# The weighting of the value rows in the softmax pass, moved from VectorE to GpSimd

## The chip, the cores and the metric

The kernel runs on one core of one Trainium2 chip. The metric is the device time of one execution in microseconds (us). A core has TensorE (PE), VectorE (DVE), ScalarE (ACT), GpSimd (POOL) and SyncE (SP, which only issues transfers here). Each engine takes its own instructions in order; engines wait for each other through semaphores. A row that begins with an engine's name and a small q (DVEq) shows the sequencer of that engine, which reads loop bounds, works out addresses and issues instructions.

## The reference, cut to what matters

A graph network over 6250 nodes and 200,000 edges that are sorted by their destination. Two convolutions come first, then attention over the edges, whose last part the change touches:

```
logits = (q[dst] * k[src]).sum(-1) * scale + (edge_attr @ ew + eb)   # 8 heads
amax = segment_max(logits, dst)
pe = exp(logits - amax[dst])
ssum = segment_sum(pe, dst)
w = pe / clip(ssum[dst], 1e-06)
o = segment_sum(w[:, :, None] * v[src], dst)                          # 8 heads x 16 columns
```

## The kernel before, in words

The kernel is a row of phases with a barrier of all engines between them: projection, convolution, node update, the same again, the projection to q, k and v, `logits_pass`, `node_maxima`, `softmax_pass`, and a last node update. The change is in `softmax_pass`, which takes the edges 512 at a time: 392 groups ("supers") of `TILES` = 4 tiles of 128 edges. The division by `ssum` is left to the last node update, so the pass sums `exp * v` (128 columns) and `exp` (8 columns) by destination node.

All engines run the same loop, written by `slots`: one turn for each super, four turns written out in an iteration (`DEPTH` = 4), so that every fourth turn has the loop's branch ahead of it. I call four turns a lap. The stages of one super lie in different turns: with lag 1 TensorE finds the maxima of its nodes, with lag 2 VectorE subtracts them, with lag 3 ScalarE takes the exponential, with lag 4 the value rows are multiplied by it, and with lag 5 the products are summed by node. An engine is in the turn that its own waits allow, so ScalarE may take the exponential of a super right after VectorE's subtraction.

What each engine does in a turn, in its order:

- TensorE: for each block of 128 nodes that the super of lag 5 touches, eight recorded matmuls (L743, four products of 128x136 in f32, each in two parts) of the one-hot matrix `hot` with `vals`; a small matmul (L749) that marks `vals` as read; then the maxima of the super of lag 1 (L1500, L663 for each block, L1504).
- VectorE: reads the super's first and last block into registers (L580, L598); for each block builds `hot` (L708, is_equal of `node_row` and `dst_cols`, both in SBUF) and adds the sums of the block before from PSUM to `acc` (L729); then reduces the maxima from PSUM (L1551), subtracts them from `logits` (L1553, both inputs in SBUF), and multiplies the value rows by their weights (L1559, `vals` from `v` and the last 8 columns of `vals`, all in SBUF).
- ScalarE: the exponential into the last 8 columns of `vals` (L1520), then for each block two passes that make the one-hot matrix `pick` for the maxima (L644, L648).
- SyncE: loads `dst` (a buffer is free when `picked` says so) and `v` (free when `vals` says so), four buffers each.
- GpSimd: one iota at the start of the pass and nothing more.

Two supers are in the sums at a time: `hot` and the PSUM bank of the sums are double. A super whose edges end in another block than they began in has two blocks (there are 47 of these); its second product waits for the second `hot` and for L729, which wait for the first product.

The semaphores that the change touches are `weight` (the exponential is there), `v_in` (the value rows have landed) and `vals` (the product is there: TensorE and SyncE wait for it).

Of the kernel before, what the change touches and what calls it, by code (L numbers as in the profile page):

```python
# [27 lines left out]
ALU = mybir.AluOpType  # L28
# [3 lines left out]
P = 128  # L32
N_NODES, N_EDGES, D = 6250, 200000, 128
HEADS, GROUPS, ED, TD = 8, 8, 4, 512
HD = D // HEADS
# [3 lines left out]
TILES = 4  # L39
# [9 lines left out]
ACC_W = D + HEADS  # L49
# [60 lines left out]
def build(nc, io, out):  # L110
    ctx = ExitStack()
    with ctx:
# [1323 lines left out]
        def softmax_pass():  # L1436

            with ExitStack() as st:
# [9 lines left out]
                dst, v = deep("dst", [P, SUPER]), deep("v", [P, TILES, D])  # L1448
                apart, picks = b("apart", [P, SUPER]), Picks("sm", b("pick", [P, 2, SUPER], BF16))
                zeros = b("zeros", [2, TILES * 3 * HEADS], BF16)  # L1450
                below, highest, vals = b2("below", [P, TILES * HEADS]), b2("highest", [P, TILES * HEADS]), deep("vals", [P, TILES, ACC_W])
# [8 lines left out]
                MAXIMUM, BELOW, LOAD_V, EXPONENT, WEIGHT, SCATTER = 1, 2, 2, 3, 4, 5  # L1460
                with nc.Block() as block:
                    @block.sync
                    def _(sp):
                        def body(stage):
                            if stage(0):
                                s, r, k = stage(0)
                                hold(sp, S["picked"], s - (DEPTH - 1), S["sp_paced"])
                                sp.dma_start(dst[r][:, :], dst_rows[bass.ds(s, 1), :].to_broadcast([P, SUPER])).then_inc(S["dst_in"][r], 16)
                            if stage(LOAD_V):
                                s, r, k = stage(LOAD_V)  # L1470

                                hold(sp, S["vals"], s - (DEPTH - 1), S["sp_paced"])
                                sp.dma_start(v[r][:, :, :], v_edges[bass.ds(s, 1), :, :].rearrange("a p (j c) -> (a p) j c", c=D)).then_inc(S["v_in"][r], 16)
                        slots(sp, LOAD_V, body)

                    @block.gpsimd
                    def _(pool):
                        number_nodes(pool, None, node_row, S["nodes"])

                    @block.tensor  # L1480
                    def _(pe):
                        picked, scattered = picks.counters(pe), scatter.counters(pe)
                        kept = span_registers(pe, "sm")

                        pe.wait_ge(S["set"], 1)
                        pe.matmul(bank(SUMS[0])[:, 0:ACC_W], hot[0][:, 0, :], vals[0][:, 0, :], start=True, stop=True).then_inc(S["sums"], 1)

                        def body(stage):

                            far = stage(SCATTER) and kept_span(pe, kept[stage(SCATTER)[1]])  # L1490
                            near = stage(MAXIMUM) and keep_span(pe, kept[stage(MAXIMUM)[1]], span("pe", stage(MAXIMUM)[0])[0])
                            if stage(SCATTER):
                                s, r, k = stage(SCATTER)
                                scatter.products(pe, scattered, far, r, vals[r], (S["vals"], s + 1))
                            if stage(MAXIMUM):
                                s, r, k = stage(MAXIMUM)

                                wait(pe, S["below"], s - 1)
                                maxima = bank(MAX[r % 2])[:, 0:TILES * 3 * HEADS]
                                pe.matmul(maxima, digit_w[:, :], zeros[:, :], start=True, stop=False, skip_group_check=True)  # L1500
                                pick_pe(pe, picks, picked, near, maxima.rearrange("p (j c) -> p j c", c=3 * HEADS),
                                        lambda blk: [max_parts[:, bass.ds(blk, 1), :, :].rearrange("p a k c -> p (a k c)")])

                                pe.matmul(maxima, digit_w[:, :], zeros[:, :], start=False, stop=True,  # L1504
                                          skip_group_check=True).then_inc(S["maxima"], 1)
                        slots(pe, SCATTER, body)

                    @block.scalar
                    def _(act):
                        picked = picks.counters(act)  # L1510
                        act.sem_inc(picks.made, 1)

                        def body(stage):
                            ends = stage(0) and span("act", stage(0)[0])[0]
                            if stage(EXPONENT):
                                s, r, k = stage(EXPONENT)
                                act.wait_ge(S["below"], s + 1)

                                wait(act, S["vals_free"], s - (DEPTH - 1))
                                act.activation(vals[r][:, :, D:ACC_W], below[r % 2][:, :].rearrange("p (j h) -> p j h", h=HEADS),  # L1520
                                               ACT.Exp).then_inc(S["weight"], 1)
                            if stage(0):
                                s, r, k = stage(0)
                                pick_act(act, S, picks, picked, ends, dst[r][:, :], apart[:, :], (S["dst_in"][r], 16 * (k + 1)))
                                act.sem_inc(S["picked"], 1)
                        slots(act, EXPONENT, body)

                    @block.vector
                    def _(dve):
                        scattered, before = scatter.counters(dve), [counter(dve, f"sm_before_{x}", 0) for x in ("block", "bank")]  # L1530
                        dve.sem_inc(picks.used, 2)
                        number_nodes(None, dve, node_row, S["nodes"])
                        dve.memset(vals[0][:, :, :], 0.0)
                        dve.memset(hot[0][:, :, :], 0.0)
                        dve.memset(zeros[:, :], 0.0).then_inc(S["set"], 1)
                        dve.memset(acc[:, :, :], 0.0).then_inc(S["sums_free"], 1)
                        dve.wait_ge(S["sums_free"], 1)

                        def body(stage):
                            if stage(SCATTER):  # L1540
                                s, r, k = stage(SCATTER)
                                scatter.names(dve, scattered, before, span("dve", s)[0], s, r, node_row)
                            if stage(BELOW):
                                s, r, k = stage(BELOW)
                                dve.wait_ge(S["maxima"], s + 1)

                                wait(dve, S["weight"], s - 1)
                                maxima = bank(MAX[r % 2])[:, 0:TILES * 3 * HEADS].rearrange("p (j k h) -> p j k h", k=3, h=HEADS)
                                under = below[r % 2][:, :].rearrange("p (j h) -> p j h", h=HEADS)

                                dve.tensor_reduce(highest[r % 2][:, :], maxima.rearrange("p j k h -> p j h k"), AX.X, ALU.add).then_inc(S["maxima_used"], 1)  # L1551
                                dve.wait_ge(S["maxima_used"], s + 1)
                                dve.tensor_tensor(under, logits[:, bass.ds(s, 1), :].rearrange("p a (j h) -> p (a j) h", h=HEADS),  # L1553
                                                  highest[r % 2][:, :].rearrange("p (j h) -> p j h", h=HEADS), ALU.subtract).then_inc(S["below"], 1)
                            if stage(WEIGHT):
                                s, r, k = stage(WEIGHT)
                                dve.wait_ge(S["weight"], s + 1)
                                dve.wait_ge(S["v_in"][r], 16 * (k + 1))
                                dve.tensor_tensor(vals[r][:, :, 0:D].rearrange("p j (h c) -> p j h c", c=HD),  # L1559
                                                  v[r][:, :, :].rearrange("p j (h c) -> p j h c", c=HD),  # L1560
                                                  vals[r][:, :, D:ACC_W].unsqueeze(3).to_broadcast([P, TILES, HEADS, HD]),
                                                  ALU.mult).then_inc(S["vals"], 1)
                        slots(dve, SCATTER, body)
                        q = value(dve, scattered[0], 1)
                        dve.wait_ge(S["sums"], q)
                        scatter.add(dve, q, before)
# [59 lines left out]
```

## Time and profile before

| | |
|---|---|
| time, median of 3 runs | 8547.21 us (8544.19 to 8551.21) |
| the profiled execution: time / span | 8545.18 / 8543.4 us |
| busy, share of the span | PE 75%, DVE 65%, POOL 54%, ACT 54% |
| softmax pass | from about 7010 to 8416 us |
| in it: PE / DVE / ACT / POOL busy | 1193.87 / 843.32 / 721.02 / 0.00 us of 1406 |
| granted TensorE clock in it | 0.50 of full speed |

Shares of the whole span mix phases with different limits, and GpSimd's 54% lies in the gathers of the convolutions and of the logits pass. The softmax pass has to be read by itself, turn by turn.

### The profile page before, as it was taken

To read this page: it belongs to the slowest core of one execution; us is meant where nothing else is said; L and a number is where in the kernel's file an instruction comes from. 1 tells how busy PE (TensorE), PEld (TensorE's weight loads), DVE (VectorE), ACT (ScalarE), POOL (GpSimd) and SP (SyncE) were. 2 spreads that over 40 slices of the span, in tenths; PEclk is the share of its full clock that TensorE was granted. 3 is DMA by queue.
4 is the path that set the end of the run, shared out by engine and by line. 5 is a ranking of instruction groups with operands and counts; after the bars stand their busy time and mean duration, and the time that the engine had idled before them with its cause. 6 is when DMAs were issued, how large, how long until landed. Compare 5 with 4: busy or idle time off the path is not lost. (4 is left out here: it accounts for less than half of the span.)

```text
span 8543.4 us, 249109 instructions
## 1 busy us (share of the span) xinstructions
PE 6370.7 (75%) x43500; PEld 4258.2 (50%) x43501; DVE 5559.4 (65%) x14407; ACT 4605.3 (54%) x7842; POOL 4629.7 (54%) x4730
## 2 busy tenths in 40 slices
PE   1788888888648888888884677777666658888884
PEld 1455555555435555555553434343333337776664
DVE  5667676777656666677776566666666666665556
ACT  3445555555334555555552567777777765555542
POOL 0777777777427777777772477777666520000000
PEclk9999999999869999999996655555555555555555
DMA  4445445555225445445451577777666545444442
GB/s 151 134 135 134 135 134 133 134 135 134 73 62 135 134 133 135 135 134 133 134 134 45 162 214 217 215 215 204 194 184 178 167 121 167 156 148 143 135 133 74
DMA packets 1002205, 1233.71 MB, mean 144 GB/s; under 512 B 305427, under 2 KB 647422, under 8 KB 1000674
## 3 DMA queue, kind: packets, MB, share of 16 engines
q1 hardware_dynamic: 776358, 718.99, 28.5%
q0 software_dynamic: 225792, 514.10, 22.5%
q8 instruction: 20, 0.33, 0.0%
q14 instruction: 35, 0.29, 0.0%
HBM read 1091.01 MB, written 141.49 MB: 144 GB/s over the span
## 5 line engine op out<-in xcount | busy, mean ns | idle before, releaser
L823 POOL DMA_INDIRECT conv_rows<-src_table,conv_idx x3136 | 3105.4, 990 | 955.2 <-issue 919.4
L1243 POOL DMA_INDIRECT lg_rows<-kv_table,lg_idx x1568 | 1482.8, 946 | 792.8 <-issue 594.2
L663 PE MATMUL ps<-dst_parts,lg_pick 128*128 x5268 | 668.3, 304 | 671.9 <-ACT lg_pick L648 668.0
L743 PEld LDWEIGHTS ps<-conv_vals,conv_hot 128*128 128x128 f32 x7024 | 916.0, 191 | 504.9 <-issue 349.7
L743 PE MATMUL ps<-sm_vals,sm_hot 128*128 128x136 f32 x3512 | 952.2, 452 | 202.9 <-DVE acc L729 137.7
L887 ACT ACTIVATE conv_sq<-ps 128x512 f32<-128x512 f32 x784 | 468.1, 597 | 1108.2 <-PE ps L853 1010.0
L663 PEld LDWEIGHTS ps<-dst_parts,lg_pick 128*128 x5268 | 522.1, 132 | 1052.3 <-issue 1021.1
L847 PE MATMUL ps<-conv_rows,ident_b 128*128 128x512 bf16 x2352 | 646.8, 384 | 523.6 <-DMA conv_rows<-src_table,conv_idx 478.3
L926 DVE TENSOR_REDUCE conv_var<-conv_sq 128x32 f32<-128x512 f32 x784 | 536.5, 684 | 760.3 <-ACT conv_sq L887 734.6
L743 PE MATMUL ps<-conv_vals,conv_hot 128*128 128x129 f32 x7024 | 938.6, 276 | 108.8 <-DVE acc L729 104.2
L1391 DVE CUSTOM_DVE_ANT_0 acc<-ps,acc 128x512 f32<-128x512 f32 x976 | 635.4, 689 | 549.9 <-ACT acc L1306 497.5
L743 PEld LDWEIGHTS ps<-sm_vals,sm_hot 128*128 128x128 f32 x3512 | 814.0, 329 | 278.9 <-DVE acc L729 213.7
L648 ACT ACTIVATE conv_pick<-conv_apart,one_col 128x512 f32 x878 | 633.7, 722 | 459.3 <-PE ps L663 307.8
L708 DVE TENSOR_TENSOR conv_hot<-conv_node_row,dst_cols 128x512 f32 (+1 forms) x878 | 605.2, 689 | 386.9 <-PE ps L743 312.8
L1306 ACT ACTIVATE acc<-ps,neg_win 128x512 f32<-128x512 f32 x976 | 622.0, 685 | 384.5 <-issue 330.8
L868 PE MATMUL ps<-conv_y,ident 128*128 128x512 f32 x1568 | 806.7, 596 | 3.6 <-DVE conv_y L956 3.6
L663 PE MATMUL ps<-dst_parts,conv_pick 128*128 x10536 | 768.9, 222 | 8.0 <-issue 3.8
L892 ACT ACTIVATE conv_vals<-ps 128x512 f32<-128x512 f32 x784 | 468.1, 597 | 405.0 <-PE ps L868 404.6
L663 PEld LDWEIGHTS ps<-dst_parts,conv_pick 128*128 x10536 | 610.0, 99 | 114.4 <-issue 24.4
L644 ACT ACTIVATE conv_apart<-conv_dst,neg_node 128x512 f32<-128x512 f32 x878 | 628.0, 715 | 40.0 <-DMA conv_dst<-dst_rows 19.9
L956 DVE TENSOR_TENSOR conv_y<-conv_y,conv_gamma 128x512 f32<-128x512 f32 x784 | 545.0, 695 | 15.0
L949 DVE TENSOR_TENSOR conv_y<-ps,conv_rstd 128x512 f32<-128x512 f32 x784 | 534.1, 681 | 0.1
(223 smaller groups left out, 9447.7 us busy)
## 6 DMA issues: line engine op xcount, KB each, us to landing
conv_dst<-dst_rows SPq DMA_DIRECT2D x784, 256.0 KB
acc<-dst_rows SPq DMA_DIRECT2D x392, 256.0 KB
v_edges<-lg_rows SPq DMA_DIRECT2D x392, 256.0 KB
sm_dst<-dst_rows SPq DMA_DIRECT2D x392, 256.0 KB, 3.3
sm_v<-v_edges SPq DMA_DIRECT2D x392, 256.0 KB, 2.6
conv_rows<-src_table,conv_idx POOLq DMA_INDIRECT x3136
conv_ea<-ea_parts SPq DMA_DIRECT2D x784, 36.0 KB
lg_rows<-kv_table,lg_idx POOLq DMA_INDIRECT x1568
```

Source lines behind the costliest of these rows:

```text
L644: act.activation(apart, dst, ACT.Square, bias=neg_node[:, bass.ds(blk, 1)]).then_inc(picks.apart_made, 1)
L648: act.activation(picks.buffer(act, turn), apart, ACT.Relu, bias=one_col[:, 0:1], scale=-1.0).then_inc(picks.made, 1)
L663: last = pe.matmul(to[:, j, :], names, part, start=False, stop=False, skip_group_check=True)
L708: dve.tensor_tensor(hot[:, :, :], node_row[:, bass.ds(blk, 1), :].to_broadcast([P, TILES, P]), dst_cols[:, bass.ds(TILES * s, TILES)].unsq ...
L743: last = pe.matmul(bank(SUMS[g])[:, 0:self.width], self.hot[g][:, j, :], vals[:, j, 0:self.width], start=(j == 0), stop=(j == TILES - 1))
L823: pool.indirect_dma_start(rows[r][:, j, :], None, src_table, bass.IndirectOffsetOnAxis(idx[r][:, j:j + 1], 0)).then_inc(S["rows_in"][r], 16)
L847: last = pe.matmul(bank(MSG[r]).rearrange("p (j c) -> p j c", c=D), ident_b[:, :], rows[r][:, :, p * D:(p + 1) * D], start=(p == 0), stop= ...
L868: pe.matmul(bank(SHIFT[r % 2]).rearrange("p (j c) -> p j c", c=D), ident[:, :], y[r % 2][:, :, :], start=False, stop=True, skip_group_chec ...
L956: dve.tensor_tensor(y[r % 2][:, :, :], y[r % 2][:, :, :], gamma[:, :].unsqueeze(1).to_broadcast([P, TILES, D]), ALU.mult).then_inc(S["gain ...
L1243: pool.indirect_dma_start(rows[r][:, j, :], None, kv_table, bass.IndirectOffsetOnAxis(idx[r][:, j:j + 1], 0)).then_inc(S["rows_in"][r], 16)
L1306: act.activation(far[h], bank(AGAIN[r % 2]), ACT.Square, bias=neg_win[:, bass.ds(w + h, 1)], scale=PEN).then_inc(S["far"], 1)
L1391: dve.tensor_tensor_reduce(masked[h], bank(SPREAD_TO[r % 2]), far[h], 1.0, NEG, ALU.subtract, ALU.max, top[:, h:h + 1]).then_inc(S["top"], 1)
```

## The change

The multiplication by the weights leaves VectorE's loop and becomes a loop of its own on GpSimd, with the same waits, operands and semaphore. GpSimd runs the stage with the other engines' lag, but nothing else is in its loop.

```diff
@@ pool
 number_nodes(pool, None, node_row, S["nodes"])
+def body(stage):
+    if stage(WEIGHT):
+        s, r, k = stage(WEIGHT)
+        pool.wait_ge(S["weight"], s + 1)
+        pool.wait_ge(S["v_in"][r], 16 * (k + 1))
+        pool.tensor_tensor(vals[r][:, :, 0:D].rearrange("p j (h c) -> p j h c", c=HD),
+                           v[r][:, :, :].rearrange("p j (h c) -> p j h c", c=HD),
+                           vals[r][:, :, D:ACC_W].unsqueeze(3).to_broadcast([P, TILES, HEADS, HD]),
+                           ALU.mult).then_inc(S["vals"], 1)
+slots(pool, WEIGHT, body)
@@ dve, at the end of its turn
-if stage(WEIGHT):
-    s, r, k = stage(WEIGHT)
-    dve.wait_ge(S["weight"], s + 1)
-    dve.wait_ge(S["v_in"][r], 16 * (k + 1))
-    dve.tensor_tensor(vals[r][:, :, 0:D].rearrange("p j (h c) -> p j h c", c=HD),
-                      v[r][:, :, :].rearrange("p j (h c) -> p j h c", c=HD),
-                      vals[r][:, :, D:ACC_W].unsqueeze(3).to_broadcast([P, TILES, HEADS, HD]),
-                      ALU.mult).then_inc(S["vals"], 1)
```

VectorE, in the middle of its loop, from the subtraction of one turn to the `hot` of the next, before:

```order
L1551 TENSOR_REDUCE sm_highest<-ps 128x32
L1553 ISA
L1553 TENSOR_TENSOR sm_below<-logits,sm_highest 128x32
L1558 REGISTER_ALU
L1559 TENSOR_TENSOR sm_vals<-sm_v,sm_vals 128x4x128
L580 ISA
L580 TENSOR_LOAD ranges
L689 ISA
L598 REGISTER_ALU
L598 UNCONDITIONAL_BRANCH
L598 ISA
L708 ISA
L708 TENSOR_TENSOR sm_hot<-dst_parts,dst_cols 128x512
```

The same place now (lines of `softmax_pass` have moved by 11):

```order
L1562 TENSOR_REDUCE sm_highest<-ps 128x32
L1564 ISA
L1564 TENSOR_TENSOR sm_below<-logits,sm_highest 128x32
L580 ISA
L580 TENSOR_LOAD ranges
L689 ISA
L598 REGISTER_ALU
L598 UNCONDITIONAL_BRANCH
L598 ISA
L708 ISA
L708 TENSOR_TENSOR sm_hot<-dst_parts,dst_cols 128x512
```

The multiplication and a register instruction are gone; the sequencer's work between the subtraction and `hot` is all still there.

GpSimd's loop of the softmax pass, of which nothing stood before (the iota was followed by the branch to the next phase):

```order
+L1485 TENSOR_TENSOR sm_vals<-sm_v,sm_vals 128x4x128 x4
+L104 UNCONDITIONAL_BRANCH
+L104 ISA
+L1484 REGISTER_ALU
+L1485 TENSOR_TENSOR sm_vals<-sm_v,sm_vals 128x4x128
+L1483 REGISTER_ALU
+L1485 TENSOR_TENSOR sm_vals<-sm_v,sm_vals 128x4x128
+L1483 REGISTER_ALU
+L1485 TENSOR_TENSOR sm_vals<-sm_v,sm_vals 128x4x128
+L1483 REGISTER_ALU
+L1485 TENSOR_TENSOR sm_vals<-sm_v,sm_vals 128x4x128
```

All 392 multiplications are now GpSimd's, and between two of them it has one register instruction and its waits.

## Rows read from the trace of the kernel before

**Rows 1.** Busy time of each engine in the softmax pass, then granted clock and DMA

```profile
7010.00:8416.00 1406.00, 1193.87 (x6436) 984.86 (x6436) 843.32 (x2055) 721.02 (x1266) 0.00 (x0) 0.50 0.45 144
```

**Rows 2.** Groups of instructions, 6700 to 8450: busy, mean ns, idle before, releasers

```profile
L743 PE MATMUL ps<-sm_vals,sm_hot 128*128 128x136 f32 x3512 | 952.2, 452 | 202.9 <-DVE acc L729 137.7 <-issue 42.1 <-DVE sm_vals L1559 15.3
L1559 DVE TENSOR_TENSOR sm_vals<-sm_v,sm_vals 128x512 f32<-128x512 f32 x392 | 270.3, 690 | 0.6 <-issue 0.6
```

**Rows 3.** Timeline of TensorE over one lap (start us, us, instruction)

```profile
7427.39 2.18 PE L743 MATMUL ps<-sm_vals,sm_hot 128*128 128x136 f32 x8 [0.64 <-DVE acc L729]
...
7429.91 0.26 PE L1504 MATMUL ps<-sm_zeros,digit_w 2*128 2x96 bf16 x1
7430.36 2.18 PE L743 MATMUL ps<-sm_vals,sm_hot 128*128 128x136 f32 x8 [0.19 <-DVE acc L729]
...
7432.87 0.26 PE L1504 MATMUL ps<-sm_zeros,digit_w 2*128 2x96 bf16 x1
7433.30 2.17 PE L743 MATMUL ps<-sm_vals,sm_hot 128*128 128x136 f32 x8 [0.17 <-DVE acc L729]
...
7436.12 2.18 PE L743 MATMUL ps<-sm_vals,sm_hot 128*128 128x136 f32 x8
...
7439.51 0.82 PE L743 MATMUL ps<-sm_vals,sm_hot 128*128 128x136 f32 x2 [0.62 <-DVE acc L729]
```

**Rows 4.** Timeline of VectorE over the same lap

```profile
7428.73 0.69 DVE L708 TENSOR_TENSOR sm_hot<-dst_parts,dst_cols 128x512 f32 x1 [0.29 <-issue]
...
7430.54 0.26 DVE L1551 TENSOR_REDUCE sm_highest<-ps 128x32 f32<-128x96 f32 x1 [0.40 <-PE ps L1504]
7430.95 0.19 DVE L1553 TENSOR_TENSOR sm_below<-logits,sm_highest 128x32 f32<-128x32 f32 x1
7431.06 0.69 DVE L1559 TENSOR_TENSOR sm_vals<-sm_v,sm_vals 128x512 f32<-128x512 f32 x1
7432.03 0.69 DVE L708 TENSOR_TENSOR sm_hot<-dst_parts,dst_cols 128x512 f32 x1 [0.28 <-issue]
...
7435.05 0.69 DVE L708 TENSOR_TENSOR sm_hot<-dst_parts,dst_cols 128x512 f32 x1 [0.29 <-issue]
...
7438.27 0.69 DVE L708 TENSOR_TENSOR sm_hot<-dst_parts,dst_cols 128x512 f32 x1 [0.62 <-issue]
```

**Rows 5.** VectorE's sequencer, line 580, from 7431.1 to 7432.3 (ns min/median/max)

```profile
L580 DVEq TENSOR_LOAD <-ranges x1: 301/301/301, 7431.2 to 7431.2; - x1
```

**Rows 6.** Timeline of ScalarE over the same lap: the exponentials

```profile
7431.18 0.23 ACT L1520 ACTIVATE sm_vals<-sm_below 128x32 f32<-128x32 f32 x1 [0.24 <-DVE sm_below L1553]
...
7434.27 0.23 ACT L1520 ACTIVATE sm_vals<-sm_below 128x32 f32<-128x32 f32 x1 [0.37 <-DVE sm_below L1553]
...
7437.41 0.23 ACT L1520 ACTIVATE sm_vals<-sm_below 128x32 f32<-128x32 f32 x1 [0.56 <-DVE sm_below L1553]
```

**Rows 7.** Timeline of all engines at the second block of a super

```profile
8318.73 0.69 DVE L708 TENSOR_TENSOR sm_hot<-dst_parts,dst_cols 128x512 f32 x1 [2.44 <-PE ps L743]
...
8319.68 2.18 PE L743 MATMUL ps<-sm_vals,sm_hot 128*128 128x136 f32 x8 [1.14 <-DVE acc L729]
```

**Rows 8.** Timeline of all engines in the first node update

```profile
2294.32 1.72 POOL L1147 TENSOR_TENSOR node_biased<-node_bias,node_held 128x896 f32<-128x896 f32 x1 [40.52 <-DVEq L1090]
...
2294.54 0.20 DVE L1092 RECIPROCAL node_share<-node_share 128x7 f32<-128x7 f32 x1
2294.78 2.21 DVE L1093 TENSOR_TENSOR node_stage<-acc,node_share 128x896 f32<-128x896 f32 x1
...
2304.70 0.17 DVE L1089 TENSOR_SCALAR node_held<-acc 128x7 f32 x1 [0.28 <-DVE node_y L1106]
2305.00 1.68 POOL L1147 TENSOR_TENSOR node_biased<-node_bias,node_held 128x896 f32<-128x896 f32 x1 [8.96 <-DVEq L1090]
2305.02 1.70 DVE L1091 TENSOR_SCALAR node_share<-acc 128x7 f32 x1
...
2307.09 1.09 DVE L1093 TENSOR_TENSOR node_stage<-acc,node_share 128x896 f32<-128x896 f32 x1
```

**Rows 9.** GpSimd's 14 multiplications (ns min/median/max, first and last start)

```profile
L1147 POOL TENSOR_TENSOR node_biased<-node_bias,node_held x14: 1681/1682/1719, 2294.3 to 4661.8; 128x896 f32<-128x896 f32 x14
```

## The prediction

> **What bounds the kernel now.** The change lives in the softmax pass alone, so I read first the busy times of that stretch: TensorE is busy 1193.87 of 1406 us at a granted clock of 0.50 (its 1.2 GHz level), VectorE 843.32, GpSimd not at all [rows 1]. The groups of instructions come next: 3512 recorded parts of products (439 products of eight parts, for 392 supers), 202.9 us of idle time before them, 137.7 of it put down to VectorE's L729; the multiplication that moves is 392 times 690 ns, 270.3 us in all [rows 2]. If those 270 us lay on the path, the kernel would gain 3%. Whether they do is a question for one lap of four turns.
>
> In the lap from 7427.39 to 7439.51, TensorE runs its products (L743) for 2.18 us, then the maxima up to L1504, 2.77 or 2.78 us from the start of L743 to the end of L1504, and begins the next products 0.1 to 0.7 us later; the lap is 12.12 us, 3.03 a turn [rows 3]. Does TensorE wait for anything in those gaps? Its product needs `hot`. At a second block, where it surely waits, L743 starts 0.26 us behind the end of `hot` (8319.42 to 8319.68) [rows 7]. In the lap the ends of `hot` lie at 7429.42, 7432.72, 7435.74 and 7438.96 and the products start at 7430.36, 7433.30, 7436.12 and 7439.51 [rows 3, 4]. That is 0.94, 0.58, 0.38 and 0.55 us; less the 0.26, `hot` comes **0.68, 0.32, 0.12 and 0.29 us early**. So nothing of VectorE holds TensorE in these turns, though L729 is named as the releaser: for a first block L743 needs the L729 of the turn before. What sets the pass is TensorE with its own issue gaps, which are long after the loop's branch (0.64) [rows 3]. But VectorE is only a little ahead.
>
> Its chain is this: L1504 ends at 7430.17 [rows 3], the reduction starts at 7430.54, the subtraction at 7430.95, the multiplication at 7431.06, `hot` at 7432.03 [rows 4], and the product that needs it at 7433.30. The chain spans two turns of TensorE, and its margin is the margin above.
>
> **What leaves VectorE.** The multiplication takes 0.69 us, but `hot` starts 0.97 us behind it, and of that 0.28 is marked as issue [rows 4]: the sequencer reads the super's range (a load of 0.30 us that starts at 7431.2) and sets up the loop [rows 5], all of it under cover of the multiplication. The change leaves these instructions where they are. With the multiplication gone the sequencer's work stands bare, so `hot` can start earlier by no more than the step from subtraction to multiplication, 0.11 us (7430.95 to 7431.06) [rows 4]. TensorE, which doesn't wait there, gains nothing from it. Gain: 0.
>
> **What GpSimd gets.** Its price per multiplication: it took 1682 ns for 128x896 f32, two inputs in SBUF, one of them repeated along the row [rows 9]. By size alone, 512 columns are 1682 x 512/896 = 0.96 us. With a fixed part as large as VectorE's (690 ns at 512, 1.09 us at 896, so 1.04 ns a column and 0.155 us fixed [rows 2, 8]) it is 1.03. I take **0.99**, well under a turn of 3.03: throughput is no issue, and `vals` is ready two turns before its product. SyncE's load of `v` waits for `vals`, which now comes earlier.
>
> **What GpSimd does to VectorE.** This is the term that decides. In the node update GpSimd multiplied from 2294.32 to 2296.04; VectorE's reciprocal ran in that time in its 0.20 us, but L1093, with two inputs in SBUF, started at 2294.78 and took 2.21 us, against 1.09 alone: it ended 0.95 us behind GpSimd's end. L1091 took 1.70 us in the next round, from 2305.02 to 2306.72, where GpSimd ended at 2306.68, while L1089 of the same shape took 0.17 [rows 8]. So such an instruction is held until GpSimd's multiplication ends, and is then done in its own time less 0.14 us. The Trainium skill (SBUF — State Buffer, Who interferes with whom) says that a DVE instruction with two SBUF inputs contends with a GpSimd instruction that reads SBUF, and that the one that issues second blocks fully; by that rule, the trace agrees (L1093, 2.21 us). `hot` (L708) and the subtraction (L1553) have two inputs in SBUF; the reduction and L729 read PSUM.
>
> Where does GpSimd's multiplication fall? It starts when the exponential is done: L1089 ended at 2304.87 and GpSimd began at 2305.00, 0.13 us later [rows 8]. The exponentials end at 7431.41, 7434.50 and 7437.64 [rows 6], so GpSimd starts at 7431.54, 7434.63 and 7437.77, ahead of `hot`'s new earliest starts (7431.92, 7434.94, 7438.16), and holds it each time. GpSimd ends 0.99 later, and `hot` 0.55 after that (0.69 less 0.14):
>
> - `hot` of 7432.03: ends at 7433.08, 0.36 late against 7432.72; 0.32 are free; 0.04 too late.
> - `hot` of 7435.05: ends at 7436.17, 0.43 late; 0.12 free; **0.31 too late**.
> - `hot` of 7438.27: ends at 7439.31, 0.35 late; 0.29 free; 0.06 too late.
> - `hot` of 7428.73: some 0.4 late; 0.68 free; nothing.
>
> Each chain spans two turns, so a lap is two chains end to end, either the first and third `hot` of this list (0.04 + 0.06 = 0.10) or the second and fourth (0.31 + 0). The larger one sets the lap: +0.31 us. There are 392/4 = 98 laps, 30 us if all are like this one. In the 47 turns in which TensorE takes two blocks of maxima it is longer while VectorE isn't; such a turn lies in two of the four chains, so about 24 laps have cover. 74 x 0.31 = 23 us, 98 x 0.31 = 30; I take **25 us**. At the two ends of GpSimd's price (0.96, 1.03) the lap gives 0.28 and 0.35, 21 to 34 us.
>
> By the Trainium skill (GPSIMD Engine Reference, Performance versus the Vector engine) a two-input elementwise instruction takes 4497 ns for 2048 columns; an estimate from that is 1.12 us for 512, with which the same lap would give 0.44 and the sum 33 to 43 us. The trace has 1.88 ns a column against the page's 2.20, so I go by the trace.
>
> **Sum.** The profiled execution took 8545.18 us; with 25 it is 8570. It lies 2 us under the median of the runs, so for the median I forecast 8547.2 + 25 = **8572 us**.
>
> **The rivals.**
>
> - *Hidden, no change.* `hot` is not held, because both its inputs repeat elements, or because GpSimd starts some 0.5 us behind ScalarE rather than 0.13, and `hot` goes first. Then nothing of the change reaches TensorE: 8547. For it: not every instruction is held (L1092 wasn't) [rows 8], and my margins are tenths of a microsecond. Against it: L1093 also repeats an input and was held.
> - *Slow GpSimd.* The rows of `v` are read in runs of 16 with the weight repeated, which no row of GpSimd shows (L1147 has runs of 128 or more). If that costs 1.4 us rather than 0.99, all four `hot` are 0.41 later: 0.45 and 0.47 make 0.92 a lap, 0.72 and 0.13 make 0.85; 98 x 0.92 = 90 us, 8637. It leaves the forecast's range at about 1.15 us, where the lap gives 0.47. Against it: VectorE's time doesn't depend on the shape of the runs (690 ns here).
> - *Faster.* The mechanism is that L729 or `hot` does hold TensorE as the releaser column says. Of 137.7 us [rows 2] the second blocks keep 47 x 1.14 [rows 7] = 54; of the 84 left, 0.11 us a turn can be had, 392 x 0.11 = 43: 8504. It decides if the margin of `hot` is zero in most turns. Against it: the gap ahead of L743 goes by the place in the lap (0.64, 0.19, 0.17, under 0.1), not by `hot`'s lead. The 15.3 us put down to L1559 [rows 2] could come back in this case too.
> - *The plain reading*, that 270 us leave a busy engine, gives 8277. VectorE is busy 60% of the pass; I give it nothing of its own.
>
> **How the numbers follow.** The forecast has 0.52, no change 0.25, slow GpSimd 0.14, faster 0.09. A measurement of this kernel can tell about 0.2% (17 us, so 8530 and 8564) from no change. A fifth of the forecast's chance lies under 8564. So slower has 0.42 + 0.14 = 0.56, same 0.25 + 0.10 = 0.35, faster 0.09. The range takes in no change (8547, less a few us of scatter) and the slow GpSimd to about 1.3 us: 8542 to 8625. It leaves out the faster case and a third of the slow one, about 0.14. The forecast's own range, all of the same sign, is 8555 to 8590.
>
> **What would show it.** In the changed profile: GpSimd's multiplication near 0.99 us, 392 times, 0.13 us behind the exponential; `hot` with a mean of about 1.2 us rather than 0.69, since the held time counts as its own (issue at 7431.92, end at 7433.08 makes 1.16); VectorE's busy time thus down by less than 270 us; the lap at 12.4 us, with longer gaps ahead of L743 where `hot` had 0.12 to spare; the reduction still on one PSUM input and at 0.26. If `hot` stays at 0.69, the hold is wrong and the time is that of before. If L743's gaps shrink, the margin was misread.

## The result, and the profile after

The change makes the kernel slower: 8579.33 us (median of 6 runs) against 8547.81 of before (6 runs), ratio 1.0035, 95% interval 1.0025 to 1.0045, 31.5 us. The forecast was 8572, 25 us slower.

The groups of instructions of the changed kernel from 6700 to 8480 us (busy, mean ns, idle before, releasers), which answer to [rows 2]:

```profile
L743 PE MATMUL ps<-sm_vals,sm_hot 128*128 128x136 f32 x3512 | 952.7, 453 | 237.5 <-DVE acc L729 175.3 <-issue 57.1 <-POOL sm_vals L1485 1.7
...
L708 DVE TENSOR_TENSOR sm_hot<-dst_parts,dst_cols 128x512 f32 x426 | 459.9, 1080 | 450.4 <-issue 330.5 <-PE ps L743 120.0
L1485 POOL TENSOR_TENSOR sm_vals<-sm_v,sm_vals 128x512 f32<-128x512 f32 x392 | 418.2, 1067 | 1024.2 <-ACT sm_vals L1531 1024.2
```

TensorE's busy time in its products is unchanged; the idle ahead of them grew from 202.9 to 237.5 us, and those 34.6 us are the whole lengthening of the softmax pass (its products start from 7015.6 to 8446.6, 1431.0 us, against 7019.9 to 8416.2, 1396.3 us before). The execution as a whole is 31.0 us longer (8576.18 against 8545.18), since it came to the pass some 4 us earlier. VectorE gave away 270 us of multiplications and won only 5559.4 - 5477.2 = 82 us of busy time, mainly because `hot` now takes 1080 ns in the mean for the same 128x512 that took 0.69 us in [rows 4]. GpSimd's multiplication takes 1067.

The timeline of the changed kernel, all engines, at the hand-over (answers to [rows 3, 4, 6]):

```profile
7429.01 2.18 PE L743 MATMUL ps<-sm_vals,sm_hot 128*128 128x136 f32 x8 [0.18 <-DVE acc L729]
7429.24 0.26 DVE L1562 TENSOR_REDUCE sm_highest<-ps 128x32 f32<-128x96 f32 x1 [0.34 <-PE ps L1515]
7429.66 0.19 DVE L1564 TENSOR_TENSOR sm_below<-logits,sm_highest 128x32 f32<-128x32 f32 x1 [0.16 <-DVE sm_highest L1562]
7429.97 0.23 ACT L1531 ACTIVATE sm_vals<-sm_below 128x32 f32<-128x32 f32 x1 [0.37 <-DVE sm_below L1564]
7430.36 1.06 POOL L1485 TENSOR_TENSOR sm_vals<-sm_v,sm_vals 128x512 f32<-128x512 f32 x1 [2.21 <-ACT sm_vals L1531]
...
7430.64 1.32 DVE L708 TENSOR_TENSOR sm_hot<-dst_parts,dst_cols 128x512 f32 x1 [0.79 <-issue]
...
7431.53 0.26 PE L1515 MATMUL ps<-sm_zeros,digit_w 2*128 2x96 bf16 x1
7432.23 2.18 PE L743 MATMUL ps<-sm_vals,sm_hot 128*128 128x136 f32 x8 [0.44 <-DVE acc L729]
```

Read it from ScalarE on. The exponential ends at 7430.20, GpSimd starts at 7430.36 and ends at 7431.42. `hot` starts at 7430.64, 0.98 behind the subtraction's start (the sequencer's bare work, marked 0.79 issue), and ends at 7431.96, 0.54 behind GpSimd's end. The product follows 0.27 later, and TensorE, ready since 7431.79, has a gap of 0.44 where this place in a lap, the turn ahead of the loop's branch, had 0.05 (7436.12 in [rows 3]). The lap that starts at 7049.49 ends at 7062.08, 12.59 us; the next one, up to 7074.58, takes 12.50. The same supers took 12.23 and 12.17 before (from 7052.44 to 7064.67 and to 7076.84); the 12.12 of [rows 3] is a short lap. In this way 97 laps of the pass can be set side by side: 24 laps of single blocks are 0.38 us longer in the mean, the 73 with a second block somewhere in them 0.34.

The count over the whole pass shows the same change of what TensorE waits for. At a second block, where a product surely waits for `hot`, it starts 0.24 to 0.27 us behind its end. Before, the first products of 389 of the 392 supers start 0.32 us or more behind the end of their `hot`; the other three lie in the last turns, where the maxima are done. In the changed kernel 322 of the 439 `hot` take over 0.75 us, and 135 first products start within 0.27 us of the end of `hot`, so they waited for it.

### The profile page after: what moved, and what is told of

Same layout as the page of the kernel before. It is cut to its first block and busy times, and to the rows that moved or that the text cites. A ratio compares the mean times of both kernels' runs of the same rounds, so it can differ in the third digit from the quotient of the medians.

```text
span 8574.3 us, 249686 instructions
## 1 busy us (share of the span) xinstructions
PE 6374.7 (74%) x43500; PEld 4263.3 (50%) x43501; DVE 5477.2 (64%) x14015; ACT 4603.9 (54%) x7842; POOL 5041.2 (59%) x5122
## 5 line engine op out<-in xcount | busy, mean ns | idle before, releaser
L743 PEld LDWEIGHTS ps<-conv_vals,conv_hot 128*128 128x128 f32 x7024 | 917.3, 192 | 504.8 <-issue 349.6
L743 PE MATMUL ps<-sm_vals,sm_hot 128*128 128x136 f32 x3512 | 952.7, 453 | 237.5 <-DVE acc L729 175.3
L1485 POOL TENSOR_TENSOR sm_vals<-sm_v,sm_vals 128x512 f32<-128x512 f32 x392 | 418.2, 1067 | 1024.2 <-ACT sm_vals L1531 1024.2
L743 PE MATMUL ps<-conv_vals,conv_hot 128*128 128x129 f32 x7024 | 939.4, 276 | 108.8 <-DVE acc L729 105.4
L743 PEld LDWEIGHTS ps<-sm_vals,sm_hot 128*128 128x128 f32 x3512 | 814.5, 330 | 313.5 <-DVE acc L729 248.9
L708 DVE TENSOR_TENSOR sm_hot<-dst_parts,dst_cols 128x512 f32 (+1 forms) x439 | 474.7, 1081 | 461.6 <-issue 338.0
```

The source lines that it names most:

```text
L708: dve.tensor_tensor(hot[:, :, :], node_row[:, bass.ds(blk, 1), :].to_broadcast([P, TILES, P]), dst_cols[:, bass.ds(TILES * s, TILES)].unsq ...
L743: last = pe.matmul(bank(SUMS[g])[:, 0:self.width], self.hot[g][:, j, :], vals[:, j, 0:self.width], start=(j == 0), stop=(j == TILES - 1))
```

## The experiments

Times are medians and ratios are to the kernel before on the same chip. "Pass" is the time from the first to the last start of L743 in the profile (before 1396.3, changed kernel 1431.0). The second group of four ran on a chip on which the kernel before takes 11432.52 us; each comparison is within the chip. The kernel before was not profiled there, but the four kernels that were have a granted clock of 0.50 in the softmax pass as well, and in pool_iota, which is as fast as before, the pass takes 1396.4 us. The mean of `hot` is that of the 426 instructions of its main form.

| kernel | median us | before us | ratio, 95% interval | pass us | mean ns of `hot` |
|---|---|---|---|---|---|
| changed | 8579.33 | 8547.81 | 1.0035, 1.0025 to 1.0045 | 1431.0 | 1080 |
| pool_later | 8559.67 | 8559.15 | 0.9999, 0.9990 to 1.0008 | 1397.9 | 792 |
| no_mult | 8562.17 | 8559.15 | 1.0004, 0.9995 to 1.0013 | 1395.6 | 692 |
| half_each | 8597.87 | 8559.15 | 1.0044, 1.0030 to 1.0058 | 1436.7 | 725 |
| pool_twice | 8587.57 | 8559.15 | 1.0031, 1.0019 to 1.0043 | 1424.5 | 1019 |
| cols_psum_dve | 11439.67 | 11432.52 | 1.0005, 0.9996 to 1.0015 | 1401.2 | 688 |
| cols_psum_pool | 11436.20 | 11432.52 | 1.0009, 0.9998 to 1.0019 | 1401.7 | 688 |
| pool_iota | 11429.99 | 11432.52 | 1.0000, 0.9988 to 1.0011 | 1396.4 | 693 |
| pool_reads | 11484.76 | 11432.52 | 1.0045, 1.0033 to 1.0057 | 1457.2 | 1193 |
| half_chained | 8558.17 | 8552.15 | 1.0004, 0.9995 to 1.0013 | 1399.6 | 734 |
| pe_wait | 8591.28 | 8552.15 | 1.0045, 1.0031 to 1.0059 | 1436.5 | 693 |
| no_mark_dve | 8549.86 | 8552.15 | 0.9997, 0.9988 to 1.0006 | 1393.6 | 693 |
| no_mark_pool | 8580.87 | 8552.15 | 1.0032, 1.0020 to 1.0044 | 1425.4 | 1041 |

The theory: `hot` has two inputs in SBUF and is held while GpSimd's multiplication reads SBUF; that makes it later than its margin. The main rival: the cost is that of a slower multiplication or of handing it to another engine.

**The same work, at another moment (pool_later).**

```diff
 pool.wait_ge(S["weight"], s + 1)
+wait(pool, S["vals_free"], s - 2)
```

> The changed kernel with one more wait: GpSimd starts a multiplication only when TensorE has finished the products of its turn (vals_free), so that it falls between `hot` and the next subtraction. Theory (the hold of `hot` costs the 31 us): GpSimd's 392 multiplications still take 1.06 us each, but `hot` is back to about 0.7 us from 1.08, the idle before L743 is back to about 203 us, and the time is that of the kernel before, 8548 (ratio to it 0.999 to 1.001). Rival (GpSimd's slower multiplication costs by itself, through `vals` coming later or through a wait of SyncE or TensorE on it): `vals` comes still later here, so at least as slow as the changed kernel, 8579 or more (1.0035 or more).

The timeline of this kernel, GpSimd and VectorE:

```profile
7449.56 0.69 DVE L708 TENSOR_TENSOR sm_hot<-dst_parts,dst_cols 128x512 f32 x1 [0.79 <-issue]
7450.30 1.06 POOL L1486 TENSOR_TENSOR sm_vals<-sm_v,sm_vals 128x512 f32<-128x512 f32 x1 [1.91 <-PE ps L749]
...
7451.48 0.19 DVE L1565 TENSOR_TENSOR sm_below<-logits,sm_highest 128x32 f32<-128x32 f32 x1 [0.16 <-DVE sm_highest L1563]
...
7452.79 0.69 DVE L708 TENSOR_TENSOR sm_hot<-dst_parts,dst_cols 128x512 f32 x1 [1.11 <-issue]
7453.04 1.36 POOL L1486 TENSOR_TENSOR sm_vals<-sm_v,sm_vals 128x512 f32<-128x512 f32 x1 [1.68 <-PE ps L749]
```

GpSimd does all 392 multiplications and works from `hot`'s end to the subtraction; the loss is gone. In the turn after the loop's branch `hot` comes later and starts first, and it is GpSimd that is held: 1.36 us from 7453.04, done at 7454.40, 0.92 behind `hot`'s end. Here the one that starts second waits. The idle ahead of L743 is 203.7 us. The rival falls: `vals` is later here than in the changed kernel. `hot`'s mean was forecast at about 0.7 us and is 0.79; its median is 693 ns, and 89 of 439 are still held, but outside the last turns no first product starts sooner than 0.43 us behind its `hot`, so none of these holds reaches TensorE.

**What the multiplication was worth on VectorE (no_mult).**

```diff
-dve.tensor_tensor(vals[r][:, :, 0:D] ..., v[r] ..., vals[r][:, :, D:ACC_W] ..., ALU.mult).then_inc(S["vals"], 1)
+for r in range(DEPTH): dve.memset(vals[r][:, :, :], 0.0)      # once, ahead of the loop
-scatter.products(pe, scattered, far, r, vals[r], (S["vals"], s + 1))
+scatter.products(pe, scattered, far, r, vals[r], (S["weight"], s + 1))
-hold(sp, S["vals"], s - (DEPTH - 1), S["sp_paced"])
+hold(sp, S["weight"], s - (DEPTH - 1), S["sp_paced"])
+sp.wait_ge(S["v_in"][r], 16 * k)
```

> The kernel before without the multiplication on any engine (it is left out: the sums use columns that are cleared once; TensorE and SyncE wait for `weight` in place of `vals`). Theory (VectorE's multiplication lies under the sequencer's work and beside a TensorE that waits for nothing): VectorE loses 270 us of busy time and the kernel gains nothing measurable, 8548 (0.998 to 1.001); `hot` starts about 0.1 us sooner behind the subtraction. Rival (the multiplication was on the path, and the hold gave back more than it): 43 us or more faster, 8505 or less (0.995).

Nothing measurable: with no multiplication anywhere the kernel takes what it did. In its group of `hot` the issue idle has taken the place of the multiplication (129.3 us before, 330.3 now):

```profile
L708 DVE TENSOR_TENSOR sm_hot<-dst_parts,dst_cols 128x512 f32 x426 | 295.0, 692 | 450.5 <-issue 330.3 <-PE ps L743 120.2
```

**Half of the tiles on each engine, twice (half_each, half_chained).**

```diff
+pool: tiles 2 to 3 -> S["vals_too"];  dve: tiles 0 to 1 -> S["vals"]
+pe.wait_ge(S["vals_too"], s + 1)
+hold(sp, S["vals_too"], s - (DEPTH - 1), S["sp_paced"])
```

> Two of the four tiles of each multiplication on GpSimd, two on VectorE, with a semaphore each. Theory: GpSimd needs about 0.55 us, starts 0.13 behind the exponential and ends near or before `hot`'s start, so `hot` is held by 0.1 us at most and the time is that of before, 8548 to 8553 (1.0000 to 1.0006). Rival (a GpSimd multiplication in each turn costs for its own sake): some half of the 31 us or more, 8563 (1.0018).

A miss: 1.0044, though `hot` is hardly held (725 ns). GpSimd's half took 622 ns, not 0.55 us. TensorE's timeline shows 0.78 and 0.27 ahead of L743 where 0.64 and 0.19 stand in [rows 3]:

```profile
7429.81 2.17 PE L743 MATMUL ps<-sm_vals,sm_hot 128*128 128x136 f32 x8 [0.78 <-DVE acc L729]
...
7432.86 2.17 PE L743 MATMUL ps<-sm_vals,sm_hot 128*128 128x136 f32 x8 [0.27 <-DVE acc L729]
```

I had added a wait to TensorE's turn (and one to SyncE's) and left it out of my sum. Two more kernels tell the wait from the half. In half_chained TensorE and SyncE wait as before:

```diff
-pe.wait_ge(S["vals_too"], s + 1)
-hold(sp, S["vals_too"], s - (DEPTH - 1), S["sp_paced"])
-dve.wait_ge(S["weight"], s + 1)
+dve.wait_ge(S["vals_too"], s + 1)
```

> The halves again, without the extra semaphore at TensorE and SyncE: VectorE waits for GpSimd's half (made two turns before, so it never stalls) ahead of its own half, and the others wait for VectorE's alone. The first try was 38 us slower than before though `hot` was hardly held (mean 0.73 us), with 0.78, 0.27 ahead of L743 where the kernel before has 0.64, 0.19. Theory (a wait more in TensorE's own instructions cost it, 0.1 us a turn): 8548 to 8556 here on the scale of before's 8548 (1.000 to 1.001). Rival (GpSimd's half costs by itself): 1.003 or more, as the first try.

**Only a wait (pe_wait).**

```diff
 if stage(SCATTER):
     s, r, k = stage(SCATTER)
+    pe.wait_ge(S["weight"], s + 1)
     scatter.products(pe, scattered, far, r, vals[r], (S["vals"], s + 1))
```

> The kernel before with one more wait in TensorE's turn, ahead of the products, for `weight`, which has been there for two turns. Nothing else changes. Theory (TensorE's own issue sets the pass, and a wait that never stalls still costs it some 0.1 us): the idle ahead of L743 grows from 203 to about 240 us and the time by 30 to 45 us, 1.0035 to 1.005. Rival (a satisfied wait is free and the first try's loss had another cause): 1.000.

Both as forecast: without the wait the halves cost nothing that can be told from zero, and the wait alone, for a semaphore that is long there, costs 39 us. Its group of products has the idle in it, and the column of releasers names a finished ScalarE for part of it:

```profile
L743 PE MATMUL ps<-sm_vals,sm_hot 128*128 128x136 f32 x3512 | 954.4, 453 | 240.3 <-DVE acc L729 166.9 <-ACT sm_vals L1521 47.0 <-DVE sm_vals L1560 16.5
```

The pass is 1436.5 - 1396.3 = 40.2 us longer, 0.10 us for each of 392 turns. So the wait costs as much as the whole change, and TensorE's issue is what this pass runs on.

**Twice the work on GpSimd (pool_twice).**

```diff
-pool.tensor_tensor(vals[r][:, :, 0:D] ..., ALU.mult).then_inc(S["vals"], 1)
+pool.tensor_tensor(vals[r][:, :, 0:D] ..., ALU.mult).then_inc(S["once"], 1)
+pool.wait_ge(S["once"], s + 1)
+pool.tensor_tensor(vals[r][:, :, 0:D] ..., ALU.mult).then_inc(S["vals"], 1)
```

> The changed kernel with each multiplication made twice on GpSimd, the second counted. Theory: GpSimd works 2.1 to 2.3 us from each exponential on. Either `hot` gets in between the two or it is held for both. Held for both, all four `hot` of a lap are about 1.1 to 1.3 us later than in the changed kernel, a lap of two chains is 2.4 us longer and the kernel about 230 us slower than the changed one, 8810 (1.03). Slipped in between, `hot` is as in the changed kernel and only the second multiplication may meet the next subtraction: 8580 to 8620. Rival (the cost is not a hold but the load of GpSimd, which is still under a turn): the same 8579.

`hot` slips in between the two, the second of the two cases:

```profile
7427.73 1.06 POOL L1485 TENSOR_TENSOR sm_vals<-sm_v,sm_vals 128x512 f32<-128x512 f32 x1 [3.74 <-ACT sm_vals L1536]
7428.20 1.14 DVE L708 TENSOR_TENSOR sm_hot<-dst_parts,dst_cols 128x512 f32 x1 [0.79 <-issue]
7428.87 1.39 POOL L1490 TENSOR_TENSOR sm_vals<-sm_v,sm_vals 128x512 f32<-128x512 f32 x1
...
7434.30 1.06 POOL L1490 TENSOR_TENSOR sm_vals<-sm_v,sm_vals 128x512 f32<-128x512 f32 x1
7434.31 1.09 DVE L1569 TENSOR_TENSOR sm_below<-logits,sm_highest 128x32 f32<-128x32 f32 x1 [0.16 <-DVE sm_highest L1567]
```

`hot` waits for the first multiplication, the second waits for `hot`, and now and then the subtraction meets one (1.09 us in place of 0.19). The time, 1.0031, can't be told from the changed kernel's. On the scale of 8548 it is 8574, a little under the 8580 to 8620 of that case and nearer to the rival's 8579. That doubled work costs no more speaks as much for the rival that a load under a turn is free as for the hold; this run alone doesn't part them.

**One input of `hot` out of SBUF (cols_psum_dve, cols_psum_pool).** The first is the kernel before with this edit, the second the changed kernel with it.

```diff
+dve.tensor_copy(cols_ps, dst_cols[:, 7 * TILES:387 * TILES])   # once, into three unused PSUM banks
 dve.tensor_tensor(hot[:, :, :], node_row[:, bass.ds(blk, 1), :].to_broadcast([P, TILES, P]),
-                  dst_cols[:, bass.ds(TILES * s, TILES)].unsqueeze(2).to_broadcast([P, TILES, P]),
+                  cols_ps[:, bass.ds(TILES * (s - 7), TILES)].unsqueeze(2).to_broadcast([P, TILES, P]),
```

> A control: the kernel before, but for 380 of 392 supers `hot` takes dst_cols from a copy in PSUM, so that it has one input in SBUF. The multiplication stays on VectorE. Both theories: 8548, if reading PSUM makes `hot` no slower (0.69 to 0.75 us; at 0.12 us and more the smallest margin is used up and the time rises a little).

> The changed kernel (multiplication on GpSimd at the same moments) with `hot`'s dst_cols from PSUM. Theory (an instruction with two inputs in SBUF is held while GpSimd reads SBUF, one with a single one isn't): `hot` takes about what it does in the control, not 1.08 us, though GpSimd still works beside it, and the time is the control's, 8548 (0.999 to 1.001 of before). Rival (any VectorE instruction suffers beside GpSimd's multiplication, or the cost is not in `hot`): `hot` stays near 1.08 us or the time near 8579 (1.0035).

Both as the theory has it. The strongest line of the study is in the second one's answer on the tile `hot` (ns min/median/max): the 426 that read PSUM are at their own 689 ns, and of the 13 whose super is at the ends and still reads SBUF most are held (median 1278), in the same pass, beside the same multiplications of 1059 ns.

```profile
L713 DVE TENSOR_TENSOR sm_hot<-dst_parts,ps x426: 686/689/690, 9918.0 to 11281.3; 128x512 f32 x142
L713 DVE TENSOR_TENSOR sm_hot<-dst_parts,dst_cols x13: 691/1278/1537, 9896.1 to 11297.8; 128x512 f32<-128x512 f32 x13
```

What these two kernels show holds for `hot`, a comparison of two tensors. That any instruction with one input in SBUF goes free, as the expectation words it, they don't show, and [rows 8] have one that doesn't: L1091, with `acc` as its only tensor, took 1.70 us there. In 11 of the 14 rounds of the node updates it took 1.69 to 1.70 us and ended 0.03 us behind GpSimd's multiplication, in the other three 0.17.

**Another load on GpSimd beside an unchanged VectorE (pool_iota, pool_reads).** The first writes only, the second reads two constant tiles; nobody waits for either.

```diff
+pool.wait_ge(S["weight"], s + 1)
+wait(pool, S["extra"], s)                                                            # its own last one
+pool.iota(extra_i[:, :], [[1, 1100]], base=0, channel_multiplier=0)                  # pool_iota
+pool.tensor_tensor(extra_o[:, :, :], iota_row[:, :].unsqueeze(1).to_broadcast([P, TILES, P]),
+                   ident[:, :].unsqueeze(1).to_broadcast([P, TILES, P]), ALU.mult)   # pool_reads
```

> The kernel before, multiplication on VectorE, and GpSimd in each turn writes an iota of 128x1100 int32 (about 1.0 us, reads nothing) once the exponential is there. Theory by the Trainium skill (SBUF — State Buffer, Who interferes with whom: a GpSimd instruction that only writes doesn't contend with two SBUF inputs): `hot` stays at 0.69 us and the time at 8548. Rival (any GpSimd instruction holds VectorE): `hot` at 1.1 us or more, 8580 or more.

> The kernel before, multiplication on VectorE, and GpSimd in each turn multiplies two constant tiles of 128x512 in SBUF (about 1 us) into a scratch tile that nobody reads, once the exponential is there. Theory: the hold alone is the cost, so it comes without moving anything: GpSimd starts behind VectorE's own multiplication, `hot` ends 0.6 us late, and the time is 8590 to 8610 (1.005 to 1.007), more than in the changed kernel. Rival (the cost comes from `vals` being made by GpSimd): 8548, since nobody waits for this.

The iota, 1045 ns in the mean, holds nothing, though 326 of the 439 `hot` start while one runs (325 start inside a multiplication in the changed kernel):

```profile
L708 DVE TENSOR_TENSOR sm_hot<-dst_parts,dst_cols x439: 691/693/695, 9920.7 to 11316.6; 128x512 f32 x142, 128x512 f32<-128x512 f32 x5
```

By the Trainium skill's rule on GpSimd instructions that only write (SBUF — State Buffer, Who interferes with whom), this trace agrees. The reading multiplication brings the loss without anything being moved, 52 us, inside the forecast of 42 to 62 (8590 to 8610 less 8548; the ratio is below 1.005 since the rest of the kernel is longer on this chip):

```profile
L708 DVE TENSOR_TENSOR sm_hot<-dst_parts,dst_cols x439: 678/1382/1691, 9889.9 to 11346.1; 128x512 f32 x142, 128x512 f32<-128x512 f32 x5
```

It is worse than the changed kernel for two reasons. Where GpSimd starts inside VectorE's own multiplication (257 times) it ends 1.13 us behind it, so it falls on `hot` later. And this multiplication is itself slower: 1.27 us in the median where it started outside one, against 1.06 in the changed kernel.

**A shorter turn for TensorE (no_mark_dve, no_mark_pool).**

```diff
-pe.matmul(bank(self.spare)[:, 0:1], ident_b[:, :], ident_b[:, 0:1], start=True, stop=True).then_inc(S["vals_free"], 1)
-wait(act, S["vals_free"], s - (DEPTH - 1))
```

> The kernel before without the small matmul L749 and ScalarE's wait for its semaphore (the subtraction that ScalarE waits for already follows a matmul that TensorE issues behind those products). Theory: TensorE's turn is the bound and gets 0.14 us shorter (L749 at 7429.36, L1500 at 7429.50), 0.56 a lap, until `hot` binds: its margins of 0.68, 0.32, 0.12 and 0.29 us shrink by 0.28 each, the smallest to minus 0.16, so the lap is 0.40 shorter, 98 times: 39 us faster, 0.9955 (between 0.9935 and 0.997). Rival (VectorE or the DMAs set the pass): 1.000.

> The changed kernel (all on GpSimd) without L749. Theory (chains of two turns, `hot` held): with `hot` 0.35 to 0.43 late by the hold and the margins 0.28 smaller, the two chains of a lap exceed TensorE's by 0.66 and 0.59, the lap is 12.22 us against 12.12 before: 0 to 15 us slower than the kernel before (1.000 to 1.002) and 45 to 60 us slower than the same kernel with the multiplication on VectorE: the harm of the hold grows when TensorE gets faster. Rival (a fixed cost of 31 us of the move): 8 us faster than before, 0.999.

A miss for the first: 0.9997, nothing gained, and so the second is much the changed kernel again, 1.0032. The timeline of TensorE in no_mark_dve shows why:

```profile
7441.72 2.17 PE L743 MATMUL ps<-sm_vals,sm_hot 128*128 128x136 f32 x8
7443.83 0.26 PE L1501 MATMUL ps<-sm_zeros,digit_w 2*128 2x96 bf16 x1
```

L1501 starts 2.11 us behind L743; with L749 between them it was 2.11 too (7430.36 and 7432.47). In the kernel before TensorE's sequencer reads the range of the next super at that place, 0.30 us from 7432.1, and L1500 follows behind it:

```profile
L580 PEldq TENSOR_LOAD <-ranges x1: 302/302/302, 7432.1 to 7432.1; - x1
7432.47 0.10 PEld L1500 LDWEIGHTS ps<-sm_zeros,digit_w 2*128 2x128 bf16 x1 [0.21 <-issue]
```

TensorE's loader has 0.21 of issue ahead of L1500 there, and 0.25 ahead of L1501 in no_mark_dve. I read from this that the small matmul had lain under the sequencer's work and was not on the path; no run here changes that work to test it. The test of the chains at a faster TensorE therefore didn't take place, and no version here is measurably faster than the kernel before.

## Why the prediction was right

- *What bounds the pass.* That TensorE waits for nothing of VectorE's, though L729 is named as the releaser of 137.7 us, is borne out by no_mult (1.0004), by pe_wait, where 0.10 us of issue a turn goes straight into the time, and by the count of first products that start 0.32 us or more behind their `hot` (389 of 392). The faster rival and the plain reading (270 us) fall with no_mult.
- *What leaves VectorE.* `hot` starts 0.98 behind the subtraction's start (7429.66 to 7430.64), where it was 1.08 (7430.95 to 7432.03): 0.10 of the 0.11 forecast, and worth nothing.
- *The hold.* Shown three ways: moved in time it vanishes (pool_later), with one input in PSUM it vanishes (cols_psum_pool), and a read that nobody needs brings it back (pool_reads). `hot` ended 0.54 us behind GpSimd's end, forecast 0.55; the product 0.27 behind `hot`, forecast 0.26. The no-change rival falls: an instruction whose inputs repeat elements is held all the same. In one point the prediction was careless: it took L1091 [rows 8] as a case of an instruction with two inputs in SBUF, and L1091 has one. Its estimate for `hot` rests on L1093 as well, which has two, so nothing in the sum changes. That each `hot` would be held, for a mean of about 1.2 us, was too much: 322 of 439 were, and the mean is 1.08.
- *Sizes.* GpSimd took 1.06 us, not 0.99 (my bounds were 0.96 and 1.03, both too low), and started 0.16 behind the exponential ahead of the `hot` that decides (0.08 ahead of the others), not 0.13. With both, that `hot` is 0.53 late rather than 0.43, and the lap 0.41 longer rather than 0.31. Measured lap against lap it is 0.38 in the laps of single blocks: the lap that I had read has one of the smaller margins (that `hot` ends 0.38 us ahead of its product in it, 0.42 in the median of the pass). The cover was wrong: I had taken the gain of 24 laps as nothing for their second blocks, but the 73 laps that have one are 0.34 longer, nearly as much as the rest. So the term of one lap was too small (0.31 for 0.38), the count of laps too (about 80 for 98), and the 25 us are short by both: 98 laps of 0.35 make the 34.7 us of the profiled pass. 31.5 were measured in the medians.
- *The slow GpSimd* of the rival (1.4 us for runs of 16) didn't come: from 896 to 512 columns it goes from 1682 to 1057 ns. The estimate from the Trainium skill (GPSIMD Engine Reference, Performance versus the Vector engine), 1.12 us, was as far above the measured 1.06 as mine was below. That the operands' pattern can matter to GpSimd is seen in pool_reads, where two repeated tiles of 128x512 take 1.27.

## What to carry to other kernels

Before moving work off a busy engine, measure how early its result is for the engine that ends last, and look at what else covers the same time: here a sequencer's register work hid the instruction, so moving it won nothing. Then look at what the new engine holds up: here a GpSimd multiplication with both inputs in SBUF stopped the VectorE instruction with two SBUF inputs that came behind it (`hot`, 0.69 to 1.08 us in the mean). Place such work in VectorE's gaps (pool_later), or take one of the two inputs from PSUM (cols_psum_pool); L1091 is a warning that one SBUF input alone is no promise. And count each wait that an edit adds to the bounding engine, even one that never stalls.

## What the runs showed that I had not expected

- A satisfied wait on TensorE costs 0.10 us a turn in this pass (40.2 us over 392), as much as the change itself.
- Taking away a matmul that the profile shows as 0.21 us busy gave nothing: the start-to-start distance (2.11 us) stayed the same, by my reading since the engine's sequencer was the slower one there.
- GpSimd's multiplications by a repeated input took 622, 1057 and 1682 ns for 256, 512 and 896 columns: 1.70 and 1.63 ns a column, which leaves about 0.2 us fixed, as an estimate from these three.
- GpSimd is held in the same way: 1.36 and 1.39 us in place of 1.06 when it came second. Held in either order, the second one ended 0.14 us sooner than its own time behind the first: `hot` 0.55 behind GpSimd, GpSimd 0.92 behind `hot`. Held time is counted as busy on both engines, so the busy share of neither says what it did.
